# A transformer tower on one core: the mean squares of its norms laid out by token, in ten columns

## The reference

```
def _layernorm(x, axis=-1, eps=1e-05):
    m = jnp.mean(x, axis=axis, keepdims=True)
    v = jnp.var(x, axis=axis, keepdims=True)
    return (x - m) / jnp.sqrt(v + eps)

h = h + _L0_attn_ref(_layernorm(h, axis=-1), ...)
h = h + _L0_ffn_ref(_layernorm(h, axis=-1), ...)
h = h + _L1_attn_ref(_layernorm(h, axis=-1), ...)
h = h + _L1_ffn_ref(_layernorm(h, axis=-1), ...)
```

## Time and profile before

| | us |
|---|---|
| median of 3 runs | 885.64 (885.04 to 885.79) |
| the profiled execution | 881.1 |
| its span | 879.4 |
| PE busy in it | 793.7 (90%), 7700 matmuls |
| DVE busy in it | 614.7 (70%) |
| ACT busy in it | 391.3 (45%) |

### The profile page before, as it was taken

The page is one execution under the profiler, slowest core; times in us unless marked ns, Lnnn a source line. Parts: engine busy times, 40 slices in busy tenths (PEclk is TensorE's granted clock), DMA queues, the critical chain, the costliest instruction groups (busy, mean ns, idle before and its releaser), DMA issues.

```text
span 879.4 us, 19821 instructions
## 1 busy us (share of the span) xinstructions
PE 793.7 (90%) x7700; PEld 586.2 (67%) x7700; DVE 614.7 (70%) x976; ACT 391.3 (45%) x561; POOL 183.5 (21%) x197
## 2 busy tenths in 40 slices
PE   4998978989986988977798998799999999999997
PEld 3665757944543666755487885477777777777775
DVE  5796697678787386898767977767777655545544
ACT  5344764610224143666457965334444432323332
POOL 7000790006999801000402420000000000000000
PEclk9999979999999999999999999799999999999999
DMA  8000000020000000010130001144444322222221
GB/s 310 1 2 1 3 1 3 3 96 1 0 0 1 0 2 1 1 39 1 37 78 14 22 21 38 57 127 158 154 150 154 109 68 57 70 69 69 68 61 51
DMA packets 24073, 46.07 MB, mean 52 GB/s; under 512 B 2605, under 2 KB 10541, under 8 KB 23629
## 3 DMA queue, kind: packets, MB, share of 16 engines
q1 hardware_dynamic: 24013, 45.21, 16.8%
HBM read 41.91 MB, written 1.36 MB: 49 GB/s over the span
## 4 chain that ended last, share of the span: by engine, by line
PE 70%; DVE 21%; ACT 4%; issue 3%; POOL 1%; DMA 1%; SPq 0%; DVEq 0%; ACTq 0%; POOLq 0%
PE psum L1790 11%; PE psum L1791 11%; PE psum L1792 11%; PE psum L1982 6%; PE psum L1992 4%; PE psum L828 4%; PE psum L829 4%; PE psum L830 4%; PE psum L2124 1%; DVE arena L1460 1%; PE psum L2170 1%; DVE arena L1658 1%; PE psum L1963 1%; PE psum L2187 1%; PE psum L2156 1%
## 5 line engine op out<-in xcount | busy, mean ns | idle before, releaser
L1790 PE MATMUL psum<-xh,arena 128*128 128x296 f16 (+1 forms) x664 | 193.3, 291 | 8.3 <-DVE xl L1333 5.0
L1791 PE MATMUL psum<-xl,arena 128*128 128x296 f16 (+1 forms) x664 | 193.2, 291 | 0.0
L1792 PE MATMUL psum<-xh,arena 128*128 128x296 f16 (+1 forms) x664 | 193.2, 291 | 0.0
L697 DVE TENSOR_TENSOR arena<-arena 128x592 f16<-128x592 f32 x68 | 52.7, 775 | 61.1 <-ACT arena L608 60.8
L603 ACT ACTIVATE arena<-psum 128x592 f32<-128x592 f32 x66 | 43.8, 664 | 115.7 <-PE psum L1792 115.7
L1790 PEld LDWEIGHTS psum<-xh,arena 128*128 (+2 forms) x664 | 65.3, 98 | 30.8 <-DVE xl L1333 4.5
L752 DVE TENSOR_TENSOR arena<-psum,arena 128x592 f32<-128x592 f32 x64 | 49.6, 775 | 50.8 <-PE psum L1792 50.6
L828 PE MATMUL psum<-arena 128*128 128x296 f16 x272 | 79.9, 294 | 4.6 <-DVE arena L697 3.8
L608 ACT ACTIVATE arena<-arena 128x592 f16<-128x592 f32 x66 | 46.0, 696 | 77.6 <-DVE arena L691 74.8
L829 PE MATMUL psum<-arena 128*128 128x296 f16 x272 | 79.9, 294 | 0.0
L830 PE MATMUL psum<-arena 128*128 128x296 f16 x272 | 79.8, 293 | 0.0
(11 more groups left out here) (321 smaller groups left out, 1675.3 us busy)
## 6 DMA issues: line engine op xcount, KB each, us to landing
arena<-comb SPq DMA_DIRECT2D x62, 296.0 KB, 3.3
arena<-in_wmoe SPq DMA_DIRECT2D x34, 384.0 KB, 3.0
arena<-in_xt SPq DMA_DIRECT2D x4, 864.0 KB, 9.6
arena<-in_w SPq DMA_DIRECT2D x2, 1024.0 KB, 6.6
arena<-arena SPq DMA_DIRECT2D x6, 187.0 KB
arena<-in_ctrl SPq DMA_DIRECT2D x1, 1056.0 KB, 9.1
out<-arena SPq DMA_DIRECT2D x2, 512.0 KB, 3.1
arena<-in_wlin SPq DMA_DIRECT2D x1, 768.0 KB, 4.4
```

What stands on the lines that cost most here:

```text
L697: dve.tensor_tensor(al[:, s_], t1, ah[:, s_], ALU.subtract).then_inc(ev["al"], 1)
L1790: pe.matmul(dst, wh, mh, start=start, stop=False)
L1791: pe.matmul(dst, wh, ml, start=False, stop=False)
L1792: return pe.matmul(dst, wl, mh, start=False, stop=stop)
```

## The change

The operands of the mean-square matmuls change places. A tile of 128 tokens of sq is now the weights and one column of `mean_ones` moves, so that the mean square of token p of tile i lands in partition p of column i. The ten tiles begin at multiples of 128, but the last begins at 1056, so that it is whole (`tile_at`). Square root and reciprocal work on 128 x 10. The spreading takes column i, broadcast over 128 columns, as weights and moves the piece of the identity that belongs to the chunk: 3, 3, 3 and 4 pieces for the four chunks (`tile_pieces`), each at most 128 columns wide. `KEEP["rec"]` goes from 16 to 5. All of this is done in ln1 to ln4 and at cv.

```diff
+def tile_at(i):
+    return min(128 * i, T - 128)
+
+
+def tile_pieces(q):
+    pieces, at = [], CH * q
+    while at < CH * (q + 1):
+        i = at // 128
+        end = min(128 * (i + 1), CH * (q + 1))
+        pieces.append((i, at - tile_at(i), at - CH * q, end - at))
+        at = end
+    return pieces
...
-KEEP = {"rec": 16, "mx1": 18, "tok": 12, ...
+KEEP = {"rec": 5, "mx1": 18, "tok": 12, ...
...
-                act.activation(sd, bank((name, "v"))[:, 0:CH], ACT.Sqrt, bias=eps[:, 0:1]).then_inc(emptied["act"], 1)
+                act.activation(sd[:, 0:NT], bank((name, "v"))[:, 0:NT], ACT.Sqrt, bias=eps[:, 0:1]).then_inc(emptied["act"], 1)
...
-                dve.reciprocal(sd, sd).then_inc(ev[name + "_rec"], 1)
+                dve.reciprocal(sd[:, 0:NT], sd[:, 0:NT]).then_inc(ev[name + "_rec"], 1)
...
+            def spread_rows(ps, q, roots):
+                for i, first, at, w in tile_pieces(q):
+                    ins = pe.matmul(ps[:, at:at + w], roots[:, i:i + 1].to_broadcast([128, 128]),
+                                    ident[:, first:first + w], start=True, stop=True)
+                return ins
...
-                for q in range(NCH):
-                    pe.wait_ge(ev[name + "_sq"], q + 1)
-                    ps = bk[32 * q:32 * q + 32, 0:CH]
-                    pe.matmul(ps, mean_ones[:, 0:32], sq[:, 0, cols(q)], start=True, stop=False)
-                    ins = pe.matmul(ps, mean_ones[:, 0:32], sq[:, 1, cols(q)], start=False, stop=True)
+                for i in range(NT):
+                    pe.wait_ge(ev[name + "_sq"], (tile_at(i) + 127) // CH + 1)
+                    for c in range(2):
+                        ins = pe.matmul(bk[:, i:i + 1], sq[:, c, tile_at(i):tile_at(i) + 128], mean_ones[:, 0:1],
+                                        start=c == 0, stop=c == 1)
...
-                    rows = slice(32 * q, 32 * q + 32)
-                    pe.matmul(fill((name, "r", q))[:, 0:CH], spread[rows], sd[rows], start=True, stop=True).then_inc(filled[who((name, "r", q))], 1)
+                    spread_rows(fill((name, "r", q)), q, sd).then_inc(filled[who((name, "r", q))], 1)
...
-            for q in range(NCH):
-                if q == 2:
+            for i in range(NT):
+                half = (tile_at(i) + 127) // (2 * CH)
+                if half and not (tile_at(i - 1) + 127) // (2 * CH):
                     keep_clock(fill(("cr", 0)), KEEP["csq"])
-                pe.wait_ge(ev["csq"], q // 2 + 1)
-                ins = pe.matmul(bk[32 * q:32 * q + 32, 0:CH], mean_ones[:, 0:32], rp[:, cols(q)], start=True, stop=True)
+                pe.wait_ge(ev["csq"], half + 1)
+                ins = pe.matmul(bk[:, i:i + 1], rp[:, tile_at(i):tile_at(i) + 128], mean_ones[:, 0:1], start=True, stop=True)
```

More of the change, by code:

```diff
@@ L206 @@
 FILLERS = 5
-KEEP = {"rec": 16, "mx1": 18, "tok": 12, "xq": 12, "mx2": 20, "hq": 12, "split": 12, "combine": 12, "op": 14, "csq": 36,
+KEEP = {"rec": 5, "mx1": 18, "tok": 12, "xq": 12, "mx2": 20, "hq": 12, "split": 12, "combine": 12, "op": 14, "csq": 36,
         "qkrec": 32, "km": 30, "on": 24}
@@ L1102, in _ @@
             full(act, ("cv",))
-            act.activation(r3[:, 0:CH], bank(("cv",))[:, 0:CH], ACT.Sqrt, scale=D / BW, bias=eps[:, 1:2]).then_inc(emptied["act"], 1)
+            act.activation(r3[:, 0:NT], bank(("cv",))[:, 0:NT], ACT.Sqrt, scale=D / BW, bias=eps[:, 1:2]).then_inc(emptied["act"], 1)
             for q in range(NCH):
@@ L1433, in _ @@
             after(dve, ("cv",))
-            dve.reciprocal(r3[:, 0:CH], r3[:, 0:CH]).then_inc(ev["crec"], 1)
+            dve.reciprocal(r3[:, 0:NT], r3[:, 0:NT]).then_inc(ev["crec"], 1)
             for q in range(NCH + 1):
@@ L1895, in _ @@
             for q in range(NCH):
-                rows = slice(32 * q, 32 * q + 32)
-                pe.matmul(fill(("cr", q))[:, 0:CH], spread[rows], r3[rows, 0:CH], start=True, stop=True).then_inc(filled[who(("cr", q))], 1)
+                spread_rows(fill(("cr", q)), q, r3).then_inc(filled[who(("cr", q))], 1)
             pe.wait_ge(ev["dwl"], 1)
```

## The result

The changed kernel takes 894.17 us (890.18 to 896.92), the kernel before, on the same chip, 885.34 (884.80 to 885.79). The ratio is 1.0096, with an interval of 1.0051 to 1.0141: slower by about one per cent, where 891.4 was forecast and slower had a chance of 0.58. That is 2.8 us above the forecast and 0.2 above the upper end of its wide range (884.2 to 894.0). The profiled execution is the one of 890.18, with a span of 888.5 (before 881.1 and 879.4). In the changed kernel the mean squares are L1835, the fillers L1810, the spreading L1815, square root and reciprocal L1080 and L1339 (at cv L1911, L1118 and L1448), DVE's product L1343 (cv L1452), xl L1347 and the products L1804 to L1806.

A forecast was written before the change was run, and what follows sets the result against it. At the five places the chain ACT, DVE, PE, DVE was taken to bound the kernel. Terms with the clock as it is gave -0.6 us, clock falls +6.4: +5.8 on 885.64, so 891.4, range 884.2 to 894.0.

The forecast's parts named there:

- The short operations: Square root 0.25 us and reciprocal 0.22 on ten columns: 2.04 us less at each of five places.
- The mean squares: Weight loads 0.111 us apart, 4.65 us a norm: 1.77 more in each of ln1 to ln4, 0.80 more at cv.
- At cv: 0.80 - 2.04 + 0.1 = -1.1 us at this place, with no new fall of the clock.
- The spreading and PE's order: DVE's product 0.90 us after the spreading starts; PE then late by 0.7 at ln1, 0.8 at ln2, 0.1 elsewhere.
- the sum with the clock as it is: All five places without new clock falls: +0.4, +0.5, -0.2, -0.2 in ln1 to ln4, -1.1 at cv; together -0.6 us.
- The clock: PEclk falls in each of ln1 to ln4, near the mean squares' end, at 1.6 us each: 6.4 us more.
- That the clock holds: Rival: PEclk stays 1.00 from mean squares to the end of the spreading; -0.6 us, 885.0; chance 0.28.
- falls in one or two norms only: Rival: the clock falls in only one or two of the four norms; +1.8 us, 887.4; chance 0.10.
- rival 4: Loads don't overlap with one-column matmuls and follow at some 0.2 us: 3.2 more a norm, 898 or more; chance 0.04.
- Rival 2: The clock holds and the lower level behind cv goes as well; -2.3 us in all, 883.3; chance 0.12.

The follow-up runs named there:

- e4_recip10: The kernel before with 5 fillers instead of 16 and the reciprocals of the five places on 10 columns alone; 873.76 us, 0.9887 of before.
- e6_half_loads: e1_wide with the norms' mean squares over only the first 128 of 256 features, 20 weight loads fewer a norm; 873.71 us, 0.9877 of before.
- e1_wide: The changed kernel with 128 columns of mean_ones moving in each mean-square matmul instead of one; 879.23 us, 0.9966 of before.
- e2_after_rec16: The changed kernel with 16 fillers instead of 5 between mean squares and spreading; 900.85 us, 1.0202 of before.

## Why the prediction was right, and where not

**The short operations** were right: 0.27 + 0.22 us for 0.25 + 0.22, at five places; e4_recip10 gave 8.8 us for the reciprocals alone.

**The mean squares** were right: 4.81 us at ln1 from the first load, 4.65 forecast, and the loads 0.111 to 0.112 apart; what was missing is the 0.25 from the first load to the second. At cv the twelve loads behind the last squares take 1.54 to the square root, as forecast. At ln3 and ln4 it is 5.95 and 7.37, with the clock lower in part of it. That two loads of 32 columns and eight of 128 led to the same 0.11 was a good sign. The runs show each of the 20 f32 matmuls as two records with a load each; why there are two they don't show. e6_half_loads confirms the cause: twenty fewer, 1.7 us less.

**The spreading and PE's order** were right in kind. With the clock held (e1_wide) DVE's first product starts 0.90 us after the spreading, as forecast. PE is late by 0.5 at ln1, where 0.7 was forecast; at ln2 the turning starts 0.7 later after the spreading than before, where 0.8 was forecast, but only 0.3 of it reaches DVE. Place by place against the kernel before, e1_wide gives +0.3, +0.2, -0.1 and -0.2 in the norms, where the sum with the clock as it is had +0.4, +0.5, -0.2 and -0.2. At cv it gives -0.9 up to DVE's last product, where -1.1 was forecast, and -1.8 by 80 us, since the kernel before then runs at 0.50 from 73.6 to 77.0 and e1_wide does not. The spans of the profiled executions differ by 2.0, the rest of it being where stretches at 0.50 fall elsewhere.

**The clock** was right in kind and mis-sized. The forecast put a fall at each of the four norms, near 40, 336, 430 and 538 us; they came at 40.2, 337.1, 432.7 and 541.9. The size, 1.6 each, took one stretch of 3.4 us. Against e1_wide they cost 1.2, 3.1, 3.1 and 4.4, together 11.9 and not 6.4, since at three of the places the lower clock stayed for 6.8 or 10.3 us, and the work in it is all PE's: the spreading, 3.09 us at the full clock, took 4.15 at ln1, 5.76 at ln2 and 4.75 at ln3 and ln4. Why it came back sooner at ln1 the runs don't show. It was dearest at ln4, where the fall met most of the mean squares' loads and the spreading too.

**At cv** the forecast was wrong. No new fall was expected, since only twelve loads stand there behind 36 fillers, yet the clock was at 0.50 from 70.9 to 77.7. That is about 2.5 us against e1_wide, and turns its -1.8 into +0.8. The kernel before lost the clock there as well, from 73.6; the fall now comes ahead of that, onto the spreading, and lasts twice as long. In e2_after_rec16 it does not come, so that a single column moves is not enough by itself to bring it at this place.

**What gave some of it back** was not in the sum: 4.2 us in two regions where before was at the lower clock and the changed kernel was not. The five places cost 13.3 us (1.4 + 0.8 + 3.4 + 3.5 + 4.2) where the forecast had 5.8. The term for the clock was 8.0 too small, 5.5 in the norms and 2.5 at cv; the rest of the sum came out within about 1 us. So the forecast of 891.4 is only 2.8 below the measured time because 4.2 of the 7.5 came back elsewhere. Its direction followed from its mechanism; its nearness was in part luck.

**The rivals.** That the clock holds, or falls in one or two norms only, is refuted by the profile, and e1_wide shows what holding it would have brought. The Trainium skill (TensorE: Matmul & The Clock Gate, Why this matters for your kernels) has the clock lost in mid-kernel by a gap in which PE idles. This case disagrees: PE is busy for 4.80 of 4.80 us ahead of the fall at 40.2. Loads that don't overlap (rival 4) are refuted too: 0.112 apart. Rival 2 had a true part: e1_wide has no stretch at 0.50 right behind cv, which is worth 0.9. The chances of the rivals add up to 0.33 for a time within two tenths of a per cent and 0.55 for slower, not quite the 0.30 and 0.58 that were stated.

## What to carry to other kernels

When a reduction is turned so that data become the weights and a single column moves, count the weight loads first; here 40 of them took back nearly all that a reciprocal on ten columns had saved. Then let as many columns move as the load hides: 128 cost 0.1 us a norm here and kept the clock, which was worth 11 us. Whether fewer would do was not tried. And where the clock falls, look at what PE moved ahead of the fall, not only at how busy it was.

## What was not expected of the hardware

- PE busy all the time with weight loads of 128 columns and matmuls of one column lost the clock in all four norms, and at cv, with twelve such loads, in two of three profiled executions; the same loads with 128 columns moving lost it at none of the five places. Weight loads alone did not keep it.
- At a clock of 0.50 weight loads follow 0.213 us apart instead of 0.112, so a stretch of loads takes almost twice its time, and the lower level lasted up to 10.3 us.
- A change in one place moves the falls in others. The kernel before took 879.99 to 887.76 us on one chip, and in the kernels compared here stretches at 0.50 came and went far from the edit (141.8, 518.9, 554.9 us). Effects of 2 us were therefore read in the timeline at their place and not in the time.
